# Three transposing steps behind the last chunk: where a two-bank rotation meets a row of score steps

## The reference, cut to what matters

```
q_full = concat([q_nope, rope(q_pe)]);  k_full = concat([k_nope, rope(k_pe)])   # 16 heads
scores = einsum('bhqd,bhkd->bhqk', q_full, k_full) * scale
scores = where(causal, -inf, scores)
attn   = softmax(scores)
out    = einsum('bhqk,bhkd->bhqd', attn, v)
return out.reshape(b, s, H * DV) @ w_o.T
```

## Time and profile before

| | us |
|---|---|
| median of 3 runs (range) | 1805.91 (1802.36 to 1807.36) |
| profiled execution, whole | 1806.03 |
| its span | 1804.3 |
| PE busy | 1608.8 (89%) |
| DVE busy | 1220.2 (68%) |
| ACT busy | 1026.9 (57%) |
| POOL busy | 302.1 (17%) |

### The profile page before, as it was taken

The page is one execution under the profiler, slowest core; times in us unless marked ns, Lnnn a source line. Parts: engine busy times, 40 slices in busy tenths (PEclk is TensorE's granted clock), DMA queues, the critical chain, the costliest instruction groups (busy, mean ns, idle before and its releaser), DMA issues. The chain is left out here.

```text
span 1804.3 us, 38201 instructions
## 1 busy us (share of the span) xinstructions
PE 1608.8 (89%) x14452; PEld 1318.3 (73%) x14452; DVE 1220.2 (68%) x2600; ACT 1026.9 (57%) x2017; POOL 302.1 (17%) x743
## 2 busy tenths in 40 slices
PE   3669999899999999999999999999965999988997
PEld 1357777777777777877887787787754778766886
DVE  3847766777677676777777777777746656576564
ACT  2336665666666566566666666656643435645573
POOL 3411112111211211121121121121110012020231
PEclk9879999999999999999999999999987999999999
DMA  8000000000000000000000000000011200000000
GB/s 231 1 0 2 2 2 1 2 2 1 1 2 1 2 2 2 1 1 2 2 2 1 2 2 1 2 1 2 2 26 49 81 0 1 1 19 21 1 21 27
DMA packets 27814, 23.54 MB, mean 13 GB/s; under 512 B 9692, under 2 KB 25180, under 8 KB 27508
## 3 DMA queue, kind: packets, MB, share of 16 engines
q1 hardware_dynamic: 22324, 14.77, 2.9%
q10 hardware_dynamic: 5312, 6.33, 1.2%
HBM read 19.00 MB, written 2.10 MB: 12 GB/s over the span
## 5 line engine op out<-in xcount | busy, mean ns | idle before, releaser
L697 ACT ACTIVATE pT_hi<-pT 128x512 f16<-128x512 f32 (+3 forms) x640 | 340.9, 533 | 366.7 <-PE pT L615 363.1
L818 DVE TENSOR_TENSOR pT_lo<-pT,pT_hi 128x512 f16<-128x512 f32 (+3 forms) x640 | 388.2, 607 | 159.1 <-ACT pT_hi L697 153.8
L806 DVE TENSOR_REDUCE cmx<-pS 128x1 f32<-128x512 f32 x576 | 347.9, 617 | 97.8 <-PE pS L602 94.2
L686 ACT ACTIVATE pr<-pS,nmx 128x512 f32<-128x512 f32 (+3 forms) x640 | 398.9, 623 | 11.1 <-DVE nmx L809 10.2
L615 PE MATMUL pT<-ident,pr 128*128 128x128 f32 x2176 | 346.2, 275 | 9.8 <-DVE pT_lo L818 6.9
L597 PE MATMUL pS<-lT_hi,qT_hi 128*128 128x512 f32 (+2 forms) x640 | 284.1, 444 | 57.9 <-ACT pr L686 49.0
L615 PEld LDWEIGHTS pT<-ident,pr 128*128 128x128 f32 x2176 | 258.2, 140 | 43.9 <-ACT pr L686 10.1
L657 PE MATMUL pO<-c_hi,pT_hi 128*128 128x65 f16 x2176 | 265.7, 194 | 1.2 <-DVE O L836 0.6
L658 PE MATMUL pO<-c_lo,pT_hi 128*128 128x65 f16 x2176 | 266.6, 193 | 0.0
L659 PE MATMUL pO<-c_hi,pT_lo 128*128 128x65 f16 x2176 | 263.7, 192 | 0.0
L602 PE MATMUL pS<-lT_hi,qT_lo 128*128 128x512 f32 (+2 forms) x640 | 257.4, 402 | 0.0
(11 more groups left out here) (243 smaller groups left out, 2510.0 us busy)
## 6 DMA issues: line engine op xcount, KB each, us to landing
X<-in_x SPq DMA_DIRECT2D x4, 512.0 KB, 6.8
wo<-in_w_o ACTq DMA_DIRECT2D x1, 2048.0 KB, 13.9
out<-X SPq DMA_DIRECT2D x8, 256.0 KB, 2.0
raw<-in_wd SPq DMA_DIRECT2D x14, 128.0 KB, 2.2
raw<-in_wg SPq DMA_DIRECT2D x13, 128.0 KB, 2.8
raw<-in_wu SPq DMA_DIRECT2D x13, 128.0 KB, 2.7
wqn<-in_w_qn ACTq DMA_DIRECT2D x1, 1536.0 KB, 17.6
raw<-in_qg SPq DMA_DIRECT2D x6, 128.0 KB, 2.5
```

The source lines that it names most:

```text
L686: act.activation(pr[:, at % RING, 0:n * P], pS[at % 4][:, 0:n * P], ACT.Exp, bias=nmx[:, p % 4:p % 4 + 1]).then_inc(sem("exped"), 1)
L697: act.activation(pT_hi[:, a % 4, 0:chunk[a][2] * P], src, ACT.Copy).then_inc(sem("t_hi"), 1)
L806: ch.inc(dve.tensor_reduce(cmx[:, p % 2, c:c + 1], pS[at % 4][:, 0:n * P], AX.X, ALU.max))
L818: dve.tensor_tensor(pT_lo[:, a % 4, 0:w], src, pT_hi[:, a % 4, 0:w], ALU.subtract).then_inc(sem("t_lo"), 1)
```

## The change

One line of `plan` changes. The number of T behind each S of a four-chunk head was one, one, none, two; it is one, none, none, three. Heads of three, two and one chunks keep theirs. No instruction is added or removed, and no buffer changes.

```diff
-                        for _ in range(min(n, 2) if last else int(k < n - 2)):
+                        for _ in range({4: (1, 0, 0, 3), 3: (1, 0, 2), 2: (0, 2), 1: (1,)}[n][k]):
                             one_behind()
                             if last and not placed:
                                 placed = True
                                 if p % HG == 3 and p // HG + 2 < NG:
                                     plan.append(("project", p // HG + 2))
```

## The result

The changed kernel takes 1732.29 us (median of 4 runs, 1732.11 to 1734.25) against 1805.66 us of before on the same chip: ratio 0.960, 95% interval 0.958 to 0.962, 73 us less. Forecast were 1796 us and a range of 1786 to 1809. The direction was right, the size seven times too small, and the place of most of it wrong.

What follows compares the result with a forecast made beforehand. TensorE, busy 89%, was held by idle waits on a round trip through ScalarE and VectorE, with no engine full. Terms 1.9 + 15.5 - 3.9 - 2.5 - 1.0 = 10.0 us off 1806.03 gave 1796.0 us, range 1786 to 1809.

Steps and rivals of the forecast that it cites:

- the change part by part: Walk through the four kinds of four-chunk head, counting waits that go or come: 10.0 us gained in all.
- Third heads: Plain four-chunk heads: S0 and S3 waits go, T3 waits for `t_lo`; 7.10 becomes 6.98 us, gain 1.9 us.
- Fourth heads and `turn`: Fourth heads: S3 comes 1.09 us earlier, and `turn` behind `project` up to 1.09 earlier; gain 15.5 us.
- The term of `turn`: Behind fourth heads: T work moved between `project` and `turn` fills TensorE's idle time; about 0.69 us per group, 11 us.
- The loss in units with `x_turn`: Three units, between `project` and `turn`: `x_norm` holds up `x_turn`, taking about 1.3 us from each, -3.9 us.
- Second heads: Second heads of groups: `o_out` ahead of T1's low half delays T3 to about 3.46 behind S3; sum -2.5 us.
- First heads: First heads of groups: 0.47 us gained before S3 and lost behind it, plus small terms; sum -1.0 us.
- `o_turn`: In seven first heads, a fourth turn in the row behind S3: 0.45 us lost each, -3.1 us.
- The heads with `y_add`: Three first heads: `y_add` now stands behind the last two maxima, not before them; +0.9 us each, +2.7 us.
- The bank wait eats it all: Rival: T3 starts 3.4 us or more behind S3 in plain heads; 18 us lost, time 1814; chance 0.11.
- `turn` doesn't come earlier: Rival: query copy or rotation starts no earlier against S0, so 11 us of gain go; time 1807; chance 0.10.
- the banks are free in time: Rival: T3 at 2.53 us behind S3 in plain and first heads, `o_out` covered; time 1780; chance 0.10.

Runs made afterwards that it cites:

- e1: Kernel before, its order kept, but ScalarE runs exponentials up to three chunks past the T just split: 1750.16 us, ratio 0.969.
- e5: Kernel before, but ScalarE runs two exponentials in place of one, once, behind `t_hi` of head 130's first chunk: 1757.75 us, ratio 0.973.
- e2: Changed kernel, but ScalarE runs an exponential behind a `t_hi` only while at most two chunks past it: 1805.26 us, ratio 1.000.
- e6: Kernel before, with one, none, none, three in fourth heads alone and exponentials up to three chunks past the T: 1736.20 us, ratio 0.962.

## Why the prediction was wrong, step by step

**What failed: the reach of the change.** The part "the change part by part" says "I walk each kind of four-chunk head; each of the 16 groups has one of each", and sums to 10.0 us. It has no term for heads 128 to 255, and took it that heads whose order stays keep their time. The runs show 50 us there, all from ScalarE's queue (e1 and e5 give it, or all but 1.3 us of it, without the new order; e2 keeps the new order and loses it). The prediction had met the mechanism: "The last exponential now follows `t_hi` of T0 and not of T1". It took this for a property of one head. It is a state of the walk, a count that each step carries on by one, and that nothing resets where the table's line changes. What should have told it is that the difference of ScalarE's queue is one piece without a break, from the second head to the end of attention; I looked at TensorE's and VectorE's pieces, which end with each head.

**The second thing missed in the same place.** Score steps waited for exponentials in the heads of three and two chunks as well. I asked for TensorE's waits only up to 725 us; beyond, 25.0 us of the same wait stood in the trace. The list of groups of the whole program had it too: 49.0 us before score steps for exponentials, of which rows 2 hold 19.4.

**Third heads: the steps as forecast, the size off, and the gain not the order's.** Forecast 6.98, measured 6.80. TensorE after the change, one head:

```profile
238.92 0.47 PE L597 MATMUL pS<-lT_hi,qT_hi 128*128 128x512 f32 x1
...
240.49 0.47 PE L597 MATMUL pS<-lT_hi,qT_hi 128*128 128x512 f32 x1
...
241.27 0.39 PE L597 MATMUL pS<-lT_hi,qT_hi 128*128 128x512 f32 x1
...
241.96 0.40 PE L597 MATMUL pS<-lT_hi,qT_hi 128*128 128x512 f32 x1
...
242.79 0.60 PE L615 MATMUL pT<-ident,pr 128*128 128x128 f32 x4
243.59 0.63 PE L615 MATMUL pT<-ident,pr 128*128 128x128 f32 x4
...
244.89 0.63 PE L615 MATMUL pT<-ident,pr 128*128 128x128 f32 x4 [0.30 <-DVE pT_lo L818]
...
245.72 0.47 PE L597 MATMUL pS<-lT_hi,qT_hi 128*128 128x512 f32 x1
```

S1, S2 and S3 run without a wait, and T3 comes 2.93 behind S3 (forecast 3.03) with the wait for `t_lo` that head 17 had shown. The low half starts 2.09 behind S3 and ends at 2.78, and T3 follows 0.15 later, the hand-off of the earlier trace rows:

```profile
243.71 0.16 DVE L809 TENSOR_REDUCE nmx<-cmx 128x1 f32<-128x4 f32 x1
244.05 0.69 DVE L818 TENSOR_TENSOR pT_lo<-pT,pT_hi 128x512 f16<-128x512 f32 x1 [0.18 <-ACT pT_hi L697]
```

The 0.18 us lie in the score steps: S2 to S3 takes 0.69 where I had 0.78, and S3 to T1 0.83 where the earlier trace rows had 0.93. I had taken the 0.93 from a score step that was itself late, and the 0.78 from one that follows a T and its V; S3 now follows a score step directly and on time. Third heads gained 5.2 us in all, not 1.9. The sum took this gain for the order's. The runs show that it is the lead's: this head takes 6.71 with the old order and the new lead (e1), and 7.22 with the new order and the old lead (e2). The sum had the lead in it unnamed, in the exponential that follows `t_hi` of T0.

**Fourth heads and `turn`: mechanism right, gain larger.** `project` stands 1.62 behind S3 (forecast 1.73) and `turn` 5.04 behind `project` (5.05), and its wait is gone from the list:

```profile
250.39 0.48 PE L576 MATMUL pQ<-W_hi,lT_hi 128*128 128x512 f32 x1
...
254.65 0.36 PE L597 MATMUL pS<-lT_hi,qT_hi 128*128 128x256 f32 x1
255.43 0.41 PE L583 MATMUL pQ<-ident,qs 128*128 128x128 f32 x2
```

The term of `turn` was 11 us; the heads with it took 55.2 and take 42.6. e6 shows that this comes with the fourth heads' order alone, and e2 that it doesn't need the lead (40.5 us there). The waits of fourth heads at S3 are the lead's, as in third heads (7.61 in e1, 8.34 in e2, from 8.01). The loss in units with `x_turn` came too: the fourth heads of the three such units took 0.66, 1.02 and 1.23 us more than before, and TensorE waits 3.6 us for `x_norm`.

**Second heads: right. First heads: sign off.** `o_out` behind the maximum holds up the first V of the group, and T3 behind it. VectorE, then TensorE, in head 25 after, against the earlier trace rows:

```profile
236.64 0.16 DVE L809 TENSOR_REDUCE nmx<-cmx 128x1 f32<-128x4 f32 x1
236.71 0.17 DVE L834 RECIPROCAL rl<-pO 128x4 f32<-128x4 f32 x1
236.92 0.42 DVE L836 TENSOR_TENSOR O<-pO,rl 128x256 f32<-128x256 f32 x1
237.26 0.68 DVE L818 TENSOR_TENSOR pT_lo<-pT,pT_hi 128x512 f16<-128x512 f32 x1
```

```profile
234.70 0.40 PE L597 MATMUL pS<-lT_hi,qT_hi 128*128 128x512 f32 x1
...
237.49 0.19 PE L657 MATMUL pO<-c_hi,pT_hi 128*128 128x65 f16 x1 [0.79 <-DVE O L836]
...
238.09 0.30 PE L615 MATMUL pT<-ident,pr 128*128 128x128 f32 x1
```

T3 comes 3.39 behind S3 (forecast 3.46). This head took 7.43 us against 7.32: a loss of 0.11 where 0.26 was forecast. Over heads 8 to 127 second heads lost 2.0 us, near the 2.5 forecast; the gain of 0.6 in the first table is the unreliable first unit. First heads were to lose 1.0 us and gained 2.4. The mis-sized term is `o_turn`: seven first heads with it were to lose 3.1 us and lost 1.1. The heads with `y_add` gained 2.6 (forecast 2.7), and the five others gained 1.0 where 0.6 was to be lost. The forecast 25 us of waits for `t_lo` came as 12.3 for `t_lo` and 17.1 for `o_out`.

**The rivals.** "The bank wait eats it all" named the place of the new wait rightly, but its condition, T3 at 3.4 or more in the plain head, didn't come (2.93). e2 does lose all of the order's gain, with heads 8 to 127 at 570.2 us against 566.4, and not by this rival either: T3 stands 2.94 behind S3 there, and plain third heads lose to the changed kernel at S2 and S3. "`turn` doesn't come earlier" and "the banks are free in time" are both out. None of the rivals held what happened, since all were drawn up inside the four-chunk heads.

Two small slips change nothing: of the two slices that I named in the earlier trace rows only the third is below nine tenths (the fourth reads 9), and half way between 1789 and the 1780 of the outer case is 1784.5, not 1786.

## What to carry to other kernels

Where queues are made by one walk with counters, a local edit of the table can shift a queue for all that follows: compare the whole queue of each engine, and where a difference does not end, the change has no end either. In an engine's queue that serves two consumers, put the item that is ready ahead of the one that must wait for its producer, and no further ahead than its own inputs exist: here, in heads 128 to 255, a lead of one cost 50 us and a lead of up to three 27. Ask for the waits of the whole program, not only of the stretch that the change names.

## What the hardware showed that I had not expected

A wait cost more than the idle time that the list gives it. Head 156 shows it like for like: before, its second score step had 0.17 us of idle time in front of it, yet it started 1.11 behind the first (865.38 - 864.27) in place of 0.78, and the T behind it 0.59 later in place of 0.48. That is 0.44 us for 0.17 listed. The first matmul of this step lasts 0.39 us in the record with the wait and 0.28 without. Some late steps carry no wait in the list at all, like S3 at 257.10 in the earlier trace rows, 1.06 behind S2 and 0.50 long; S3 of the changed kernel lasts 0.40.

In heads 128 to 255 the idle time before score steps that the change removed was 30.1 us by the list, while the heads got 50.5 us shorter. TensorE's idle time of all kinds fell by 23.7 us there (from 33.8 to 10.1, since waits before `x_turn` and others grew), and 26.8 us stood as busy time (566.2 us before, 539.4 after, for the same work but for a few instructions at the ends).
